# Attention with batch normalisation on one core: 32-wide contexts and Wo tiles, eight rotating PSUM banks, contexts to applications in groups of three pairs

## What is computed

```python
q = proj(Wq); k = proj(Wk); v = proj(Wv)      # each (16, 8 heads, 16, 256)
k = jax.nn.softmax(k, axis=-2)                # over the 16 channels of a head
context = jnp.einsum('bhdn,bhen->bhde', k, v)
out = jnp.einsum('bhdn,bhde->bhen', q, context)
out = jnp.einsum('oc,bchw->bohw', Wo, out.reshape(Bb, Cc, Hh, Ww))
y = out + x
mean, var = over images and pixels, for each channel
result = (y - mean) * rsqrt(var + EPS) * gamma + beta
```

## Time and profile before

| | us |
|---|---|
| median of 3 runs | 49.64 (49.45 to 49.71) |
| the profiled execution | 49.98 |
| its span, first to last instruction | 48.7 |
| TensorE busy in the span | 37.5 (377 matmuls) |
| VectorE | 34.5 |
| ScalarE | 27.1 |
| GpSimd | 18.5 |

### The profile page before, as it was taken

The page is one execution under the profiler, slowest core; times in us unless marked ns, Lnnn a source line. Parts: engine busy times, 40 slices in busy tenths (PEclk is TensorE's granted clock), DMA queues, the critical chain, the costliest instruction groups (busy, mean ns, idle before and its releaser), DMA issues.

```text
span 48.7 us, 1096 instructions
## 1 busy us (share of the span) xinstructions
PE 37.5 (77%) x377; PEld 32.5 (67%) x377; DVE 34.5 (71%) x90; ACT 27.1 (56%) x61; POOL 18.5 (38%) x28
## 2 busy tenths in 40 slices
PE   3999996869999999999999999999999930000000
PEld 3999994668887689898888979788787910000000
DVE  0019399799999958984996799793636697998000
ACT  0933550999787991593388079844634942910000
POOL 5830027399999959853017006281000000000000
PEclk9999999999999999999999999999999999555555
DMA  0398789710000000000000000000000000089995
GB/s 0 95 275 299 276 272 372 285 64 0 0 13 0 0 0 0 0 0 7 0 13 7 0 0 0 0 0 0 0 0 0 13 0 0 0 317 396 397 393 219
DMA packets 2597, 4.52 MB, mean 93 GB/s; under 512 B 416, under 2 KB 1184, under 8 KB 2592
## 3 DMA queue, kind: packets, MB, share of 16 engines
q1 hardware_dynamic: 2448, 4.33, 24.8%
q10 hardware_dynamic: 144, 0.13, 0.8%
HBM read 2.36 MB, written 2.10 MB: 91 GB/s over the span
## 4 chain that ended last, share of the span: by engine, by line
PE 59%; DVE 12%; DMA 12%; ACT 3%; SPq 3%; issue 2%; ACTq 0%
PE banks L425 17%; DMA x_sb<-x_dram 12%; PE banks L498 10%; PE banks L450 10%; PE banks L465 10%; PE banks L482 8%; DVE y_sb L407 7%; PE banks L479 4%; SPq L215 3%; DVE stats L380 3%; ACT x_hi L277 1%; DVE mean_var L389 1%; ACT v_sb L288 1%; ACT probs L282 1%; ACT std L309 1%
## 5 line engine op out<-in xcount | busy, mean ns | idle before, releaser
L263 POOL TENSOR_TENSOR probs<-probs,k_inv 128x256 f32<-128x256 f32 (+1 forms) x11 | 8.9, 822 | 8.6 <-DVE k_inv L354 8.6
L255 POOL TENSOR_TENSOR x_lo<-x_sb,x_hi 128x512 fp32r<-128x512 f32 (+1 forms) x7 | 7.8, 1124 | 5.2 <-ACT x_hi L277 5.2
L425 PE MATMUL banks<-wkv_hi,x_hi 128*128 128x256 f32 x32 | 7.2, 306 | 0.6 <-ACT v_sb L288 0.6
L277 ACT ACTIVATE x_hi<-x_sb 128x256 fp32r<-128x256 f32 (+1 forms) x11 | 5.4, 512 | 3.8 <-DMA x_sb<-x_dram 3.8
L425 PE MATMUL banks<-wkv_hi,x_lo 128*128 128x256 f32 x32 | 6.7, 290 | 0.5 <-POOL x_lo L255 0.5
L335 DVE TENSOR_REDUCE k_max<-banks 128x16 f32<-128x256 f32 (+1 forms) x11 | 5.7, 528 | 1.6 <-PE banks L425 1.5
L298 ACT ACTIVATE a_hi<-banks 128x256 fp32r<-128x256 f32 (+1 forms) x9 | 3.3, 361 | 6.2 <-PE banks L482 6.2
L425 PE MATMUL banks<-wkv_lo,x_hi 128*128 128x256 f32 x32 | 6.5, 283 | 0.0
L348 DVE TENSOR_REDUCE k_sum<-probs 128x16 f32<-128x256 f32 (+1 forms) x11 | 5.6, 532 | 0.5 <-ACT probs L282 0.4
L425 PEld LDWEIGHTS banks<-wkv_hi,x_hi 128*128 128x128 f32 x32 | 4.9, 192 | 1.5 <-issue 1.1
L342 DVE TENSOR_TENSOR probs<-banks,k_max 128x256 f32<-128x256 f32 (+1 forms) x11 | 5.6, 529 | 0.0
(11 more groups left out here) (42 smaller groups left out, 57.7 us busy)
## 6 DMA issues: line engine op xcount, KB each, us to landing
x_sb<-x_dram SPq DMA_DIRECT2D x5, 256.0 KB, 5.8
out_dram<-y_sb SPq DMA_DIRECT2D x2, 512.0 KB, 3.0
out_dram<-y_sb SPq DMA_DIRECT2D x3, 256.0 KB, 3.1
x_sb<-x_dram SPq DMA_DIRECT2D x1, 512.0 KB, 6.9
x_sb<-x_dram SPq DMA_DIRECT2D x2, 128.0 KB, 2.5
out_dram<-y_sb SPq DMA_DIRECT2D x2, 128.0 KB, 2.0
w_sb<-w_dram ACTq DMA_DIRECT2D x1, 128.0 KB, 2.7
w_sb<-w_dram SPq DMA_DIRECT2D x1, 128.0 KB, 5.7
```

The lines of the kernel that those rows point to most:

```text
L255: nc.gpsimd.tensor_tensor(x_lo[:, p, px], x_sb[:, p, px], x_hi[:, p, px].bitcast(F32), ALU.subtract).then_inc(x_lo_ready, hi - lo)
L263: nc.gpsimd.tensor_tensor(heads, heads, inv.to_broadcast([128, (hi - lo) * CH * HEADS, D]), ALU.mult).then_inc(probs_ready, hi - lo)
L277: nc.scalar.activation(x_hi[:, p, px], x_sb[:, p, px], ACT.Copy).then_inc(x_hi_ready, hi - lo)
L425: last = nc.tensor.matmul(kv_ps(p)[:, g, :], xs[:, p, g * 128:(g + 1) * 128], ws[:, :], start=start and g == CH * image, stop=stop, skip_g ...
```

## The change

The parts:

- T becomes 32: `context` has four column tiles for each image and chunk, and `times_wo` works on 32x32 tiles. For the first image of a pair they lie on the diagonal of the array. The second image's contexts are put 32 partitions further on, and its Wo products use a copy of Wo.T with its rows turned by 32 (`woT_turned`, 64 KB more in the second weight transfer), so that they lie on other tile positions; the two images' u stand in two banks (`u_ps`).
- Every PSUM use has a bank of its own by written tables (`KV_BANK`, `CT_BANK`, `A_BANK`, `Y_BANK`), all eight banks in rotation.
- No pair from the context on is divided any more; images 0, 1, 14 and 15 alone are single in the softmax stages (before: 0 to 3, 14 and 15), and `count_y` has 8 pieces instead of 9. `split_lo` of images 2 and 3 moves from VectorE to GpSimd.
- The order is written out as a list of calls for each engine. From pair 2 on, contexts, Wo products, Wq products and applications go in groups of three pairs. Waits for banks stand in TensorE's list.
- In memory, x and the result are arranged by pairs (8, 128, 512) instead of (128, 16, 256); the rearranging is outside the timed program.

```diff
-T = 64
+T = 32
-EXTRA = 2
-LAST = PAIRS - 1
-IN_PSUM = PAIRS - 3
-LO_BY_VECTOR = 2
+KV_BANK = [1, 2, 6, 7, 4, 5, 0, 1, 6, 7, 3, 4, 1, 2, 6, 7]
+CT_BANK = {0: 3, 2: 5, 4: 0, 6: 3, 8: 5, 10: 5, 12: 1, 14: 4}
+A_BANK = {0: 2, 2: 4, 4: 1, 6: 2, 8: 6, 10: 6, 12: 2, 14: 3}
+Y_BANK = {0: 0, 2: 4, 4: 0, 6: 3, 8: 7, 10: 0, 12: 7, 14: 4}
+SPLIT_BY_VECTOR = 2
+COUNTS = 8
+COPIED = 10
...
-        w_sb = sb("w_sb", [C, 4 * C])
+        w_sb = sb("w_sb", [C, 5 * C])
+        woT_turned = w_sb[:, 4 * C:5 * C]
...
+        def u_ps(lo, hi):
+            used = u_banks(lo, hi)
+            if hi - lo == 1:
+                return banks[:, used[0]:used[0] + 1, 2 * T:2 * T + C]
+            return banks[:, used[0]:used[1] + 1:used[1] - used[0], 2 * T:2 * T + C]
...
-                sp.dma_start(out[:, lo:hi, :], y_view[:, lo:hi, :]).then_inc(stored, 16)
+                sp.dma_start(in_memory(out, lo, hi), in_sbuf(y_sb, lo, hi)).then_inc(stored, 16)
...
+            def context(lo, hi):
+                pe.wait_ge(probs_ready, hi)
+                pe.wait_ge(v_ready, hi)
+                for image in range(lo, hi):
+                    ct = ct_ps(lo, hi)[:, (image - lo) * T:(image - lo + 1) * T]
+                    for g in range(CH):
+                        for t in range(0, C, T):
+                            to = (t + (image - lo) * T) % C
+                            last = nc.tensor.matmul(ct[to:to + T, :], v_sb[:, image * CH + g, t:t + T],
+                                                    probs[:, image * CH + g, t:t + T], start=(g == 0),
+                                                    stop=(g == CH - 1), tile_position=(0, to), skip_group_check=True)
+                last.then_inc(ct_ready, hi - lo)
...
+                for image in range(lo, hi):
+                    u = u_ps(lo, hi)[:, image - lo, :]
+                    wo = woT_turned if image > lo else woT
+                    for t in range(0, C, T):
+                        to = (t - (image - lo) * T) % C
+                        last = nc.tensor.matmul(u[to:to + T, :], ct_sb[t:t + T, image, :], wo[t:t + T, :],
+                                                start=True, stop=True, tile_position=(t, to), skip_group_check=True)
+                last.then_inc(u_ready, hi - lo)
...
-            run_slots((project, 0, SOFTMAX), (times_wo, 4, CONTEXT, 0, 1), (context, 3, CONTEXT),
-                      (times_wq, 4, CONTEXT), (apply, 5, CONTEXT), (times_wo, 3, CONTEXT, 1, PAIRS))
+            project(0)
...
+            project(6)
+            pe.wait_ge(v_ready, 1)
+            project(7)
+            context(0, 2)
+            pe.wait_ge(v_ready, 4)
+            project(8)
+            project(9)
+            times_wo(0, 2)
+            pe.wait_ge(v_ready, 6)
+            context(2, 4)
+            times_wq(0, 2)
+            project(10)
+            project(11)
+            pe.wait_ge(v_ready, 8)
+            apply(0, 2)
+            project(12)
...
+            project(15)
+            pe.wait_ge(v_ready, 12)
+            times_wo(2, 4)
+            pe.wait_ge(y_copied, 2)
+            context(4, 6)
+            context(6, 8)
+            pe.wait_ge(u_copied, 4)
+            context(8, 10)
+            times_wq(2, 4)
+            pe.wait_ge(v_ready, 14)
+            times_wo(4, 6)
+            times_wo(6, 8)
+            pe.wait_ge(v_ready, 15)
+            times_wo(8, 10)
+            times_wq(4, 6)
+            times_wq(6, 8)
+            pe.wait_ge(a_lo_ready, 4)
+            apply(2, 4)
+            times_wq(8, 10)
+            apply(4, 6)
+            apply(6, 8)
+            pe.wait_ge(v_ready, 16)
+            apply(8, 10)
+            context(10, 12)
+            context(12, 14)
+            pe.wait_ge(y_copied, 4)
+            context(14, 16)
+            times_wo(10, 12)
+            times_wo(12, 14)
+            pe.wait_ge(y_copied, 8)
+            times_wo(14, 16)
+            times_wq(10, 12)
+            times_wq(12, 14)
+            times_wq(14, 16)
+            apply(10, 12)
+            pe.wait_ge(y_copied, 10)
+            apply(12, 14)
+            apply(14, 16)
```

More of the change, by code:

```diff
@@ L167, in attention_batchnorm @@
         y_view = y_sb[:, :, :].rearrange("c p (b n) -> c (p b) n", n=N)
[L169 to L182, removed]
@@ new lines, in piece_of, with kv_ps, ct_ps @@
+        def piece_of(image):
+            return next(i for i, (lo, hi) in enumerate(PIECES) if lo <= image < hi)
+        def kv_ps(lo, hi):
+            if hi - lo == 1:
+                return banks[:, KV_BANK[lo], :].rearrange("n (g c) -> n g c", g=CH)
+            return banks[:, KV_BANK[lo]:KV_BANK[lo + 1] + 1:KV_BANK[lo + 1] - KV_BANK[lo], :].rearrange(
+                "n i (g c) -> n (i g) c", g=CH)
+        def ct_ps(lo, hi):
+            return banks[:, CT_BANK[lo], 0:(hi - lo) * T]
@@ new lines, in scalar_program @@
+            exponentials(0, 1)
+            copy_values(0, 1)
+            split_hi(5, 6)
+            copy_values(1, 2)
+            exponentials(1, 2)
+            split_hi(6, 8)
+            exponentials(2, 4)
+            copy_values(2, 4)
+            split_hi(8, 10)
+            exponentials(4, 6)
+            copy_values(4, 6)
+            split_hi(10, 11)
+            split_hi(11, 12)
+            split_hi(12, 14)
+            split_hi(14, 15)
+            split_hi(15, 16)
+            copy_u(0, 2)
@@ new lines, in scalar_program @@
+            exponentials(6, 8)
+            copy_values(6, 8)
+            split_a_hi(0, 2)
+            exponentials(8, 10)
+            copy_values(8, 10)
+            copy_y(0, 2)
+            exponentials(10, 12)
+            copy_values(10, 12)
+            copy_u(2, 4)
+            copy_values(12, 14)
+            exponentials(12, 14)
+            copy_values(14, 15)
+            split_a_hi(2, 4)
+            copy_u(4, 6)
+            exponentials(14, 15)
+            copy_u(6, 8)
+            copy_u(8, 10)
@@ new lines, in vector_program @@
+            shift_keys(0, 1)
+            largest_keys(1, 2)
+            shift_keys(1, 2)
+            sum_heads(0, 1)
+            invert_sums(0, 1)
+            largest_keys(2, 4)
+            sum_heads(1, 2)
+            shift_keys(2, 4)
+            largest_keys(4, 6)
+            invert_sums(1, 2)
+            shift_keys(4, 6)
+            sum_heads(2, 4)
+            invert_sums(2, 4)
+            sum_heads(4, 6)
+            mask_context(0, 2)
+            invert_sums(4, 6)
+            largest_keys(6, 8)
@@ L410, in tensor_program, with project @@
         def tensor_program(pe):
[L411 to L413 removed]
+            def project(image):
+                if image == 0:
                     pe.wait_ge(w_hi_ready, 1)
[L415 to L437 removed]
@@ L439, in context, with pass_over @@
-            def context(p, lo, hi):
-                pe.wait_ge(probs_ready, 2 * p + hi)
-                pe.wait_ge(v_ready, 2 * p + hi)
-                if p >= 1:
-                    pe.wait_ge(ct_masked, 2 * p)
-                for image in range(lo, hi):
-                    ct = ct_ps(p, lo, hi)[:, (image - lo) * T:(image - lo + 1) * T]
+                pe.wait_ge(x_hi_ready, image + 1)
+                def pass_over(xs, ws, start, stop):
+                    for g in range(CH):
+                        last = nc.tensor.matmul(kv_ps(image, image + 1)[:, g, :], xs[:, image, g * 128:(g + 1) * 128],
+                                                ws[:, :], start=start and g == 0, stop=stop, skip_group_check=True)
+                    return last
```

395 lines of the change are left out of this document (223 added, 172 removed).

## The result

The changed kernel takes 47.42 us (median of 4 runs, 47.01 to 47.87) and the kernel before, on the same chip, 49.67 (4 runs, 49.45 to 49.76): a ratio of 0.953 with a 95% interval of 0.945 to 0.961. It is faster, and within the range, but by 2.2 us instead of 5.2. The profiled execution takes 47.87 us, with a span of 46.6; it is the slowest of the four, 0.45 us above the median.

A forecast was written before the change was run, and what follows sets the result against it. TensorE, never idle from 10.16 to 38.70 us, was taken as the bound; -1.5-1.4-2.1-0.2+0.1 = -5.1 us, but walking both written lists engine by engine gave -5.3, which was used: 44.4 us, range 43.4 to 47.8.

The forecast's parts named there:

- Contexts: 32-column context blocks on four column tiles: 0.28 us a pair instead of 0.466, -1.5 us in all.
- Wo products: 32x32 Wo tiles, eight side by side: 0.265 us a pair instead of 0.44, -1.4 us in all.
- Grouping: Contexts and Wo products of three pairs together: less filling, draining and entering of tile blocks, -2.1 us.
- A: Rival on TensorE's tile blocks: records start strictly in program order, so Wo products take 0.88 a pair; 50.7 us, chance 0.11.
- C: Rival on Wo products: they stay at 0.44 a pair, two images' tiles not side by side; 45.8 us, chance 0.20.
- B: Rival on TensorE's records: a floor of 0.029 us each gives 50.7 us, the skill page's floor near 49.3; chance 0.07.
- D: Rival on tile blocks: four tiles no better than two, only grouping and start count; 47.3 us, chance 0.13.
- Start: TensorE's early waits: eight banks let image 6 start sooner, its third pass near 10.42; -0.2 us.
- Waits inside the groups: Last group's hand-overs: mask hidden, first copy of u not quite covered; +0.1 us, bounds 0 and +0.8.
- End: Last statistics in one piece of 512 columns instead of two of 256: 0 us (-0.1 to +0.3).
- Transfers: Loads and stores with x and the result arranged by pairs: 0 us, with ±0.4.
- Less work for VectorE: Narrower masks, x_lo of pair 1 moved, pairs handled whole: about 1.8 us less work, given nothing in the sum.

The follow-up runs named there:

- the kernel without the stop: The changed kernel with 14 warm-up products of 64 columns with 64-column weights in place of 7 of 128: 46.29 us, ratio 0.924.

## Why the prediction was right or wrong

**Contexts, -1.5: right.** 0.39 a block and 1.00 a group, where 0.28 + 0.155 and three times 0.28 + 0.16 were put. **Wo products, -1.4: right in time, half wrong in cause.** 0.38 a block and 0.93 to 1.05 a group against 0.95, and eight records run side by side as was put. But 64x64 tiles, turned, do as well, so the 32x32 tiles were not needed for it. **Grouping, -2.1: right** within what the groups show: all tile blocks together took 9.6 us before (eight times 0.62 + 0.58) and would take 5.7 now without the stop, 3.9 less, where the sum has 1.5 + 1.4 and 1.2 for filling and draining. No rival held: A would have given 1.7 and 2.8 us for the two groups, C 1.5 for three Wo products, B and D longer contexts. That the measured 47.42 lies beside D's 47.3, and inside the range, is chance: D's tile blocks did not come, and two losses that the forecast had not put stand in their place. B's 49.3 is also too low for its own terms: the sum gives 49.64 + 2.7 - 2.3 = 50.0, and 49.5 with the 0.5 that the walk takes off for A.

**Two steps failed, of about 1.3 us each: the sum had no term for TensorE's supply of instructions, and the term "Start" had the wrong size and sign.** The first was left out because the sum let TensorE's time go down to what its tiles need, while the number of its records went from 377 to 566. The block of pairs 2 to 4 takes from 24.02 to 26.38 with the stop and from 23.74 to 24.79 without: 2.36 against 1.05, so 1.3 us. The views of before had a trace of it in three instruction packets, none of which held TensorE up.

**"Start", -0.2, was wrong: 11.72 instead of 10.42, 1.3 us.** The term took the landing of images 6 and 7 (8.42) and added ScalarE's split and GpSimd's. It left out what stands ahead on both engines. On GpSimd these are 2.59 us for x_lo of four single images and the normalisation's 0.63, all behind images 2 and 3, which landed at 6.50. On ScalarE, images 6 and 7, landed at 7.79 in this trace, had their turn only at 8.94:

```profile
8.94 0.63 ACT L289 ACTIVATE x_hi<-x_sb 128x512 fp32r<-128x512 f32 x1
```

After it, at 9.57, GpSimd still took 0.8 us to come to them. The prediction noted that x_lo of pair 1 leaves VectorE, and counted it for VectorE only; it did not count it on the queue that it moves to. The experiments show in addition that this lateness is shared with VectorE and ScalarE, so no other order of GpSimd tried here gives it back.

**"Waits inside the groups", +0.1, was too small and in another place.** The last group has none between its stages (33.11 to 33.13 in the chain), and 0.1 inside its Wo products, busy 1.03 us where the group of pairs 2 to 4 takes 0.94 without the stop. The first single pair waits 0.31 us for the copy of u (16.27), and image 8's third pass 0.16 for x_lo (13.99 instead of 13.59 + 0.24).

**"End", 0, and "Transfers", 0: right.** From the last pass (36.69 + 0.24) to the end of the statistics (35.94 + 1.89) are now 0.90 us. Before, the last pass was

```profile
39.13 0.28 PE L498 MATMUL banks<-x_hi,a_lo 128*128 128x256 f32 x1
```

so from 39.13 + 0.12 to 38.73 + 1.37 0.85 us: no change. From there to the span's end it takes 8.8 us, 0.2 more than before (40.10 to 48.7), within the ±0.4.

Together: TensorE's last pass ends at 36.93 where 34 was forecast; 1.3 of the 2.9 is the start, 1.3 the stop, and the rest, 0.3, is of the size of the two waits. In the kernel without the stop it ends at 35.27, 1.3 after the forecast: the start again (11.50 against 10.42) and 0.2. There ScalarE is the next to bound: the chain leaves TensorE for its queue from 22.2 to 24.8, for 0.12 us of idle time so far.

**VectorE nearly without idle** did not come: it is busy 19.2 of the 22 us from 8 to 30, and 20.7 without the stop. **Steady starts in fours** did, 0.03 us apart. **Less work for VectorE** was 1.4 us (34.5 to 33.1), not 1.8.

The version to keep is the changed kernel with 14 warm-up products of 64 columns: 46.29 us, a ratio of 0.924 to the kernel before where the changed kernel has 0.953. What starts the instruction packet is open. When it began, 427 to 429 of TensorE's instructions had started in the four traces with 28 more in the list, 489 with 16 more, 581 to 625 with none more or 12 fewer. These counts are no single place in the list. In the four traces with none more or 12 fewer, an 8 KB instruction packet of another queue (q14) starts 0.3 to 0.6 us ahead of it; with 16 or 28 more that packet comes after it. Whether the one holds up the other was not tried.

## What to carry to other kernels

When a change multiplies small matmuls, count TensorE's instructions and look in the trace for an "issue" gap without a semaphore, together with a transfer of kind "instruction" just ahead of it; here 28 cheap instructions more early on took the stop away and 1.2 us with it, and 120 matmul records fewer took the stop away and 0.7 us, with slower contexts in part of the kernel. When work is moved off an engine for its relief, add it to the queue of the engine that gets it, with everything that stands ahead there. A faster block also uncovers what it used to cover: try the parts apart, in the order in which they will stand.

## What the runs showed of the hardware that was not expected

TensorE stopped after exactly 705 recorded instructions in five kernels, for 0.36 to 1.37 us from record to record, until 1.2 to 1.4 us after a 16 KB instruction packet had ended. Where the packet ended 1.7 us or more ahead of instruction 705, it did not stop (nine traces).

Eight 32x32 tiles of two images start almost together. The Wo group of the changed kernel, up to 32.17, 32.22 and 32.29:

```profile
32.08 0.34 PE L568 MATMUL banks<-w_sb,ct_sb 32*32 32x128 f32 x8
...
32.08 0.40 PE L568 MATMUL banks<-w_sb,ct_sb 32*32 32x128 f32 x9
...
32.08 0.45 PE L568 MATMUL banks<-w_sb,ct_sb 32*32 32x128 f32 x16
```

Eight have started by 32.14 already, no ninth by 32.17, and sixteen by 32.29. Records, of which a call has two, thus run eight side by side, 0.11 us a round for 128 columns. With the four diagonal tiles alone the same 16 records of a pair took 0.57 us a block instead of 0.38.
